# Semaphore raises carried by VectorE's own instructions, and a sort, a weighing and sums in smaller pieces, in a four-layer graph network kernel

## What is computed

```python
h = relu(layernorm(x)); x = x + relu(norm_adj @ (h @ W0))            # layer 0, D^-1/2 (A+I) D^-1/2
h = relu(layernorm(x)); x = x + cat(h, g@h, g@g@h, g@g@g@h) @ W.T + b # layer 1, g likewise
h = relu(layernorm(x)); x = x + mlp(h + quantile_agg(h, dilate(adj))) # layer 2
h = relu(layernorm(x)); x = x + adj @ (h @ W3) + b3                   # layer 3
```

## Time and profile before

| | |
|---|---|
| median of three runs | 1851.67 us (1849.76 to 1852.83) |
| the profiled execution: its own time, its span | 1848.78 us, 1847.0 us |
| PE busy | 1377.5 us (75%) |
| DVE busy | 1471.5 us (80%) |
| ACT busy | 826.6 us (45%) |
| POOL busy | 1304.7 us (71%) |

### The profile page before, as it was taken

How to read it: one execution, slowest core, us unless ns; L and a number is a source line. 1 busy time by engine, 2 the same in 40 slices (tenths; PEclk the granted TensorE clock), 3 DMA queues, 4 the chain that set the end, 5 groups by cost and what they waited for, 6 DMA issues and landing times.

```text
span 1847.0 us, 26217 instructions
## 1 busy us (share of the span) xinstructions
PE 1377.5 (75%) x8997; PEld 802.5 (43%) x8997; DVE 1471.5 (80%) x2491; ACT 826.6 (45%) x2340; POOL 1304.7 (71%) x1196
## 2 busy tenths in 40 slices
PE   2878768797878788787979788787979788780404
PEld 1454435455444455445444444444544545440202
DVE  1345788889898898889898888889898988988352
ACT  5354436354454646354544546354553546230202
POOL 2027787877777777878777777778787777878720
PEclk9888869797988979797988989797988879795555
DMA  4123433324333343325344334324343433222220
GB/s 143 57 54 83 71 80 64 59 60 97 58 75 81 64 92 63 71 47 98 58 75 81 69 87 64 76 44 95 59 74 82 71 86 31 28 31 28 26 15 6
DMA packets 106625, 120.25 MB, mean 65 GB/s; under 512 B 71486, under 2 KB 71614, under 8 KB 106430
## 3 DMA queue, kind: packets, MB, share of 16 engines
q0 software_dynamic: 36864, 37.82, 20.1%
q1 hardware_dynamic: 69566, 79.98, 13.7%
HBM read 109.27 MB, written 8.45 MB: 64 GB/s over the span
## 4 chain that ended last, share of the span: by engine, by line
DVE 53%; POOL 16%; issue 12%; PE 9%; ACT 6%; DMA 4%; DVEq 1%; POOLq 0%; SPq 0%; ACTq 0%
POOL slots L436 15%; DVE lists L1281 6%; DVE slots L1101 5%; DVE slots L1100 5%; PE ps_tr L687 3%; DMA slots<-h_rows,row_no 3%; DVE slots L1176 2%; DVE stat_norm L1076 2%; DVE low L1093 2%; DVE y_mid L1092 2%; ACT h L524 2%; PE ps_tr L695 2%; ACT z_mid L514 1%; DVE y_mid L1323 1%; PE ps_prod L706 1%
## 5 line engine op out<-in xcount | busy, mean ns | idle before, releaser
L436 POOL DMA_INDIRECT slots<-h_rows,row_no x1152 | 1292.9, 1122 | 459.3 <-issue 349.0
L687 PE MATMUL ps_tr<-adj_t,y_mid 128*128 128x512 bf16 x1024 | 278.6, 415 | 44.2 <-DVEq L1094 41.5
L495 ACT ACTIVATE columns_t<-ps_tr 128x512 f32<-128x512 f32 (+1 forms) x160 | 93.2, 591 | 337.5 <-PE ps_tr L695 289.7
L1100 DVE TENSOR_TENSOR slots<-slots 128x512 f32<-128x512 f32 (+3 forms) x160 | 174.7, 1092 | 63.4 <-DMA slots<-h_rows,row_no 53.5
L514 ACT ACTIVATE h<-x,stat_norm 128x64 f32<-128x64 f32 x384 | 128.0, 335 | 142.1 <-DVEq L1078 142.1
L687 PEld LDWEIGHTS ps_tr<-adj_t,y_mid 128*128 128x128 bf16 x1024 | 100.3, 105 | 198.1 <-issue 124.2
L1101 DVE TENSOR_TENSOR slots<-slots 128x512 f32<-128x512 f32 (+3 forms) x160 | 173.3, 1083 | 0.0
L1281 DVE MAX8 lists<-ps_key 128x8 f16<-128x1024 f32 x128 | 157.8, 1233 | 17.9 <-DVE lists L1281 0.5
L660 PE MATMUL ps_tr<-ident_h,adj_n 128*128 128x128 f16 x1024 | 102.3, 266 | 80.0 <-ACT adj_t L495 40.3
L695 PE MATMUL ps_tr<-adj_t,low 128*64 128x512 bf16 x1024 | 141.6, 400 | 0.0
L549 ACT ACTIVATE merged<-xc 128x256 f32<-128x256 f32 (+2 forms) x48 | 24.2, 505 | 249.8 <-DVEq L1153 249.6
(11 more groups left out here) (210 smaller groups left out, 2546.6 us busy)
## 6 DMA issues: line engine op xcount, KB each, us to landing
adj_f<-in_adj SPq DMA_DIRECT2D x128, 512.0 KB, 4.8
slots<-h_rows,row_no POOLq DMA_INDIRECT x1152, 3.1
x<-in_x SPq DMA_DIRECT2D x16, 256.0 KB, 3.0
h_rows<-h SPq DMA_DIRECT2D x16, 256.0 KB, 4.0
out<-x SPq DMA_DIRECT2D x16, 256.0 KB, 2.6
xc<-in_L_gnn_W SPq DMA_DIRECT2D x1, 64.0 KB
w_sb<-in_L_gnn_W SPq DMA_DIRECT2D x2, 32.0 KB
h_rows<-zeros SPq DMA_DIRECT2D x2, 32.0 KB, 1.5
```

The source lines that it names most:

```text
L436: pool.indirect_dma_start(out=slots[:, slot_of(par, s), t * C:(t + 1) * C], out_offset=None, in_=table[par][:, :], in_offset=bass.Indirect ...
L495: act.activation(dst, view, ACT.Copy, scale=scale).then_inc(tr_free, 1)
L687: nc.tensor.matmul(dst[:, :], top_halves(pair_of)[:, j, :], adj_t[g % 3][:, columns[j]], start=(j == 0 and not begun), stop=False)
L1100: st.done(v.tensor_tensor(low_to, first, second, ALU.min))
```

## The change

Three things change, all of them for DVE's stream; the other engines only wait on other semaphores or counts.

- In all places but `merge` (and the branch `slow_v`, which is not taken for these inputs), the separate `sem_inc` is gone, and the instruction itself raises the semaphore of the other engine in place of `v_step`. Where DVE's next instruction needs the result, DVE now waits on that other semaphore (`key_read`, `product_read`, `wide_ready`, `slots_read`, `misc_free`); elsewhere it doesn't wait at all. Two double raises become one: `flag_ready` and `result_ready` vanish (their readers use `key_free` and `prod_free`), and `aggregate` raises only `agg_ready`.
- `sort_1` and `sort_2` of `THE_REST` run as `NARROW_2` (256 columns) and `WIDE` (128 columns) one after the other. The later stages still take `THE_REST` whole.
- `weigh_odd` and `weigh_even` take three slots in three instructions of 128 x 512, which took one of 128 x 1536; the first sum of `narrow_sum` likewise.

```diff
-        NARROW_1, THE_REST = slice(0, F // 2), slice(F // 2, COLS * C)
+        NARROW_1, NARROW_2, WIDE = slice(0, F // 2), slice(F // 2, F), slice(F, COLS * C)
+        THE_REST = slice(F // 2, COLS * C)
...
             def store_result(g):
-                sp.wait_ge(result_ready, g + 1)
+                sp.wait_ge(prod_free, PROD["lin3", g] + 1)
...
             def hidden_rows(g, i):
+                if i == 0:
+                    pe.wait_ge(agg_ready, g + 1)
                 misc_turn(f"hid.{i}", g)
...
             def norm_begin(name, g):
                 total, less_mean, _, _ = stat_of(name)
                 step(v.tensor_reduce(total, tiles(x[g % 4]), AX.X, ALU.add))
-                step(v.tensor_scalar(less_mean, total, -1.0 / C, None, ALU.mult))
-                dve.sem_inc(mean_ready, 1)
+                v.tensor_scalar(less_mean, total, -1.0 / C, None, ALU.mult).then_inc(mean_ready, 1)
...
-                step(v.tensor_tensor(last[:, :, 0:C], rest, tops[:, :, C:2 * C], ALU.subtract))
-                dve.sem_inc(parts_ready, 1)
+                v.tensor_tensor(last[:, :, 0:C], rest, tops[:, :, C:2 * C], ALU.subtract).then_inc(parts_ready, 1)
...
-            def weigh(g, first, n, wire, gap):
+            def weigh(g, at, rank):
...
             def weigh_odd(g):
-                weigh(g, 2, 3, 1, 2)
+                weigh(g, 2, 1)
+                weigh(g, 3, 3)
+                weigh(g, 4, 5)
...
-                odd, even = wires(par, 2, 3, 1, F_COLS), wires(par, 10, 3, 1, F_COLS)
-                step(v.tensor_tensor(odd, odd, even, ALU.add))
                 one, two, three, last = [wires(par, s, 1, 1, F_COLS)[:, 0, :] for s in (2, 3, 4, 15)]
+                for odd, at in ((one, 10), (two, 11), (three, 12)):
+                    st.done(v.tensor_tensor(odd, odd, wires(par, at, 1, 1, F_COLS)[:, 0, :], ALU.add))
+                st.wait()
...
+            def key_read(name, g):
+                dve.wait_ge(key_free, KEY[name, g] + 1)
...
             def row_list(g, t):
-                step(v.max(out=lists[:, t * SLOTS:(t + 1) * SLOTS], in_=read_key(f"row{t}", g)))
-                free_key()
+                v.max(out=lists[:, t * SLOTS:(t + 1) * SLOTS], in_=read_key(f"row{t}", g)).then_inc(key_free, 1)
...
             def add_layer3(g):
                 dve.wait_ge(prod_full, PROD["lin3", g] + 1)
-                step(v.tensor_tensor(x[g % 4][:, :], x[g % 4][:, :], ps_prod[:, :], ALU.add))
-                dve.sem_inc(prod_free, 1)
-                dve.sem_inc(result_ready, 1)
+                v.tensor_tensor(x[g % 4][:, :], x[g % 4][:, :], ps_prod[:, :], ALU.add).then_inc(prod_free, 1)
...
-                    sort_1(c, THE_REST)
-                    sort_2(c, THE_REST)
+                    sort_1(c, NARROW_2)
+                    sort_1(c, WIDE)
+                    sort_2(c, NARROW_2)
+                    sort_2(c, WIDE)
```

More of the change, by code:

```diff
@@ L87, in gnn_stack @@
     MISC = numbered(turns, [("c", "spread"), ("c", "hid.0"), ("c", "hid.1"), ("c", "mlp")])
+    MISC_FREED = numbered(turns, [("c", "hid.0"), ("c", "hid.1"), ("c", "mlp")])
     PROD = numbered(turns, [("d", "lin3"), ("b", "lin0"), ("b", "lin1"), ("b", "v1"), ("b", "v2"), ("b", "v3")])
@@ L651, in misc_turn @@
             def misc_turn(name, g):
-                at_least(pe, misc_free, MISC[name, g])
+                at_least(pe, misc_free, MISC_FREED[name, g])
             def transpose_adjacency(g):
@@ L782, in spread_wide @@
                 pe.wait_ge(wide_summed, g + 1)
-                misc_turn("spread", g)
+                misc_turn("hid.0", g)
                 for t in range(T):
@@ L798, in slow_pe @@
             def slow_pe(g):
-                pe.wait_ge(flag_ready, g + 1)
+                pe.wait_ge(key_free, KEY["over", g] + 1)
                 settle(pe)
@@ L981, in slow_v @@
             def slow_v(g):
-                dve.wait_ge(flag_ready, g + 1)
+                dve.wait_ge(key_free, KEY["over", g] + 1)
                 settle(dve)
@@ L1166, in wide_sum @@
                 step(v.tensor_copy(parts_w[:, 1, :], agg_w[:, :]))
-                step(v.tensor_tensor(parts_w[:, 2, :], agg_w[:, :], parts_w[:, 1, :], ALU.subtract))
-                dve.sem_inc(wide_summed, 1)
-            def weigh(g, first, n, wire, gap):
+                v.tensor_tensor(parts_w[:, 2, :], agg_w[:, :], parts_w[:, 1, :], ALU.subtract).then_inc(wide_summed, 1)
+            def weigh(g, at, rank):
                 par = g % 2
                 if par:
[L1173 to L1176, removed]
+                    rank = SLOTS - 1 - rank
+                values = tiles(wires(par, at, 1, 1, slice(0, F))[:, 0, :])
+                w = weight[g % 2][:, 0:T, rank]
+                st.done(v.tensor_tensor(values, values, over_c(w), ALU.mult))
             def weigh_odd(g):
-                weigh(g, 2, 3, 1, 2)
+                weigh(g, 2, 1)
+                weigh(g, 3, 3)
+                weigh(g, 4, 5)
             def weigh_even(g):
-                weigh(g, 10, 3, 2, 2)
+                weigh(g, 10, 2)
+                weigh(g, 11, 4)
+                weigh(g, 12, 6)
             def weigh_last(g):
-                weigh(g, 15, 1, 7, 1)
+                weigh(g, 15, 7)
             def narrow_sum(g):
@@ L1267, in wide_lists @@
                                      lost.unsqueeze(1).to_broadcast([P, LIST, 2 + SLOTS]), ALU.is_equal))
-                step(v.tensor_tensor(over_b[:, :], crowd[:, :], over[:, :], ALU.add))
-                dve.sem_inc(over_ready, 1)
+                v.tensor_tensor(over_b[:, :], crowd[:, :], over[:, :], ALU.add).then_inc(over_ready, 1)
                 st.done(v.tensor_copy(lists[:, COLS * SLOTS:COLS * SLOTS + 1], self_mask[:, 0:1]))
@@ L1313, in weights, with product_read @@
                                      scale[:, :].unsqueeze(2).to_broadcast([P, COLS, SLOTS]), ALU.mult))
+            def product_read(name, g):
+                dve.wait_ge(prod_free, PROD[name, g] + 1)
             def layer0_out(g):
                 dve.wait_ge(prod_full, PROD["lin0", g] + 1)
-                step(v.scalar_tensor_tensor(y, by_tile(ps_prod), 0.0, over_c(d0[g % 2]), ALU.max, ALU.mult))
-                dve.sem_inc(prod_free, 1)
+                v.scalar_tensor_tensor(y, by_tile(ps_prod), 0.0, over_c(d0[g % 2]), ALU.max, ALU.mult)\
+                    .then_inc(prod_free, 1)
+                product_read("lin0", g)
                 step(v.tensor_tensor(tiles(x[g % 4]), tiles(x[g % 4]), y, ALU.add))
@@ L1322, in propagate @@
                 dve.wait_ge(prod_full, PROD[name, g] + 1)
-                step(v.tensor_tensor(y, by_tile(ps_prod), over_c(d1_sq[g % 2]), ALU.mult))
-                dve.sem_inc(prod_free, 1)
+                v.tensor_tensor(y, by_tile(ps_prod), over_c(d1_sq[g % 2]), ALU.mult).then_inc(prod_free, 1)
+                product_read(name, g)
                 split(y_mid, low)
```

71 lines of the change are left out of this document (31 added, 40 removed).

## The result

| | before | after |
|---|---|---|
| median of the timed runs | 1850.7 us | 1778.8 us |
| ratio, 95% interval | | 0.961 (0.959 to 0.963) |
| profiled execution: span | 1847.0 us | 1773.8 us |
| first start of a gather issue | 123.4 us | 121.8 us |
| mean of a gather issue | 1122 ns | 1061 ns |

Forecast were 1774 us and a range of 1744 to 1815 us. The page of the kernel after, the busy line and the group of the gather; they answer to the earlier trace rows. Lines of the code have moved by a few numbers (the gather is L437, the row lists are still L1281).

What follows compares the result with a forecast made beforehand. POOL's gather and DVE together set a 103.23 us turn. Fourteen turns at 98.3 us save 69.0, then 2.5 + 1.0 + 3.4 + 0.4: -76.3 from 1848.78, 1772.5, taken as 1774 us, range 1744 to 1815 us.

Steps and rivals of the forecast that it cites:

- Both engines set the turn: POOL's gather and DVE both run almost without pauses at 103.23 us a turn, so a gain on one alone stops.
- The raises, -8.9 us of a DVE turn: Removing 45 separate raises at 42 places of DVE's turn shortens the pauses: 1.2, 7.4 and 0.3 us.
- the pieces, +0.9: On DVE, splitting two sort stages, the weighings and the sum into smaller instructions adds 0.9 us a turn.
- DVE's busy share: Sign in the profile after: DVE's busy share above 84%, where it was 80% before.
- What becomes late next, 1.8 us: New DVE waits for ACT's norm (0.7 us), layer 3's split and layer 1's output (0.4 each), and layer 1's first products.
- The holds: A gather issue starting under a DVE instruction with two SBUF tensors waits for its end, then needs 0.82 us.
- The formula for a random start: Mean hold by DVE instruction length L is (L - 0.1)^2 / 2.86; the pieces cut 6.7 to 3.3 us a gather.
- The calculation issue by issue: Walking 72 issues through the new turn's 165 DVE instructions by the 0.82 rule: 96.8 to 99.5 us, middle 98.1.
- The term for the first turn's gather: The first turn's gather, with no sort beside it, was to save 1 us.
- POOL does keep the gain: Rival, 12 in 100: DVE finishes early but pieces do not help POOL; turn 101.2 to 103 us, total 1820 us.
- PE and ACT did not take over: Rival, 13 in 100: DVE's waits on PE or ACT grow to 4 us a turn; turn 100 to 101, total 1803 us.
- Slower by step: Rival, 4 in 100: in the full-width sort, four 1.22 us pieces in a row each hold an issue 1.0 us; 1867 us.

Runs made afterwards that it cites:

- experiments 1 to 4: Parts of the change added to the kernel before: raises alone 0.990, pieces alone 1.003, raises with weighing and sum pieces 0.976, raises with sort pieces 0.972.
- raises: The changed kernel with sort, weighing and sum whole again, so only the raises carried by the instructions: 1830.8 us, 0.990 of the kernel before.
- experiment 5: Against the kernel with the raises alone, two three-slot weighings became reductions reading one SBUF tensor, the six-rank weighing left out: 1831.3 us, ratio 0.990.
- pieces: The kernel before with the smaller sort, weighing and sum instructions and nothing else, all raises separate: 1855.6 us, ratio 1.003.
- finest: The changed kernel with sort_1 and sort_2 in 128-column pieces throughout, full-width stages 3, 4, middle and 5 in 256 and 128 columns: 1758.3 us, ratio 0.950.

## Why the prediction was right

*Both engines set the turn.* Shown by experiments 1 to 4, with a sign for each half: 0.990 for one, 1.003 for the other, 0.961 for both.

*The raises, -8.9 us of a DVE turn, and the pieces, +0.9.* The gaps came as worked out (0.04 and -0.08 for 0.03 and -0.08), and a stage in pieces takes 3.72 us as summed. Over the fourteen turns DVE's turn without its wait for the gather is 103.2 - 1.1 = 102.1 us before, 102.3 - 7.8 = 94.5 in `raises` and 98.4 - 3.1 = 95.3 in the changed kernel; forecast were 97.0. Less the waits for PE and ACT (0.3, 2.0 and 1.9 us) that is -9.3 us for the raises and +0.9 for the pieces, as summed. The 97.0 were too long mostly because the sum started at the whole 103.2, DVE's 1.1 us of waiting for the gather included. One sign was missed: DVE's busy share was to pass 84% and is 82%. Two instructions that overlap by 0.08 us are busy only once in that time, and by an estimate from the 32 such places, 32 x 16 x 0.08, this takes 41 us off.

*What becomes late next, 1.8 us.* Measured 1.9 us a turn, but only partly where the forecast put it, so the total is in part luck. The split of layer 3 waits 0.38 us for ACT, as forecast (0.4). The norm's wait for ACT was to cost 0.7 and costs 0.1; DVE waits 0.75 us before that, for PE's next key matrix at the row list, and ACT is done by the time that is over.

*The holds.* The rule held for the instructions with two SBUF tensors: an issue is held by one, to its end, and needs 0.82 us from there. An instruction with one tensor holds nothing in the cases forecast, with the exception in experiment 5. The formula for a random start gives 3.4 us a gather for the pieces, and in `raises` against the changed kernel the turn differs by 3.8 us. The size was close by luck more than by right: summed from the traces, the seven long instructions held the issues for 4.5 us a gather, where the formula has 6.7, and what replaced them for 1.1, where it has 3.3. Both are 2.2 too high, and only the difference is right. The issues beside the two sorts in pieces run in step with them and are free but for one (last section), which a random start does not give, and experiment 5 shows that holds do not add. The calculation issue by issue, which keeps the order, gave 98.1 us a turn; 98.4 was measured. For the raises alone it gave 101.1 and 102.3 was measured, so it is good to about 1 us in 100.

*The sum.* Forecast against measured, in spans: the 14 turns -69.0 and -67.2 (1445.3 less 1600.39 - 222.32); up to the sort of batch 0 -3.5 and -1.9; the last gather -3.4 and -3.3 (103.0 and 99.7); the tail -0.4 and -0.8 (74.5 and 73.7). In all -76.3 and -73.2. The 3.1 us that are missing are 1.8 in the turns (98.4 for 98.3), 0.9 up to the first gather (1.6 for 2.5), 0.7 from there to the first sort and 0.1 in the last gather, less 0.4 that the tail gave beyond its term. The term for the first turn's gather had no ground: 94.2 us before and 94.3 after, where the sum had 1 us less. There is no full-width sort beside it, and the sum had allowed for a gain all the same.

*The rivals.* POOL does keep the gain of the raises, all but 19 us, if it is given them alone: this rival was right about the mechanism, and the pieces are what decided against it. PE and ACT did not take over. Slower by step did not come: instructions of 1.22 us do hold single issues (in the narrow sort, which the change left as it was, the one at 704.51 takes 1.97 us, and in ten of eleven turns the first issue beside the full-width pieces is held, see the last section), but not four in a row, and the pieces hold for less in all than the whole ones did. The rule of the Trainium skill (VectorE: DVE Perf Modes, section Rules for kernel authors), "Minimize op count, not sems", is half right here: the ten more instructions a turn do cost time where DVE is the longer one (`pieces`, 1.003), but so do separate raises (without them `raises` has 0.990).

## What to carry to other kernels

Where two engines are both without pauses, measure a change of one only together with what it lets through on the other: the same edit was worth +5 us alone and -52 us on top of its partner. Beside a GpSimd that issues indirect DMAs without a pause, as here, a VectorE instruction with two SBUF tensors can hold an issue for up to its own length, so cut the longest first, and stop when VectorE waits for the gather hardly any more: the further pieces of `finest` brought nothing. Read from the timeline which instructions hold, and do not go by the number of tensors alone. Let the instruction itself raise the other engine's semaphore: a separate raise is a pause of 0.11 to 0.12 us each here.

## What was not expected of the hardware

The hold moves. With the holds at two weighings gone entirely, the kernel took as long (1831.3 against 1830.8 us), since the freed issues arrived under other instructions; after halving one of these, 9.7 us were gained.

The hold has an edge at the start. In `raises` the second weighing of the turn catches no issue that begins with it, but is a little longer itself:

```profile
766.04 1.83 DVE L1175 TENSOR_TENSOR slots<-slots,weight 128x1536 f32<-128x1536 f32 x1
```

```profile
766.08 0.95 POOL L437 DMA_INDIRECT slots<-h_rows,row_no  x1 [0.30 <-issue]
```

The first weighing takes 1.75 us, this one 1.83. Over the twelve traces, of 214 issues that begin up to 0.03 us behind the start of an instruction with two SBUF tensors (and 0.25 us or more before its end) 4 are held, and of 665 that begin 0.06 to 0.13 us behind it all are; in between it goes both ways. In the kernel before, an issue falls 0.03 to 0.05 us behind the start of the second weighing in 15 turns. It is the one behind the issue that the first weighing held, so a hold in one place decides what the next place catches.

The issues can run clear of a dense stretch: from 715.54 to 723.98 us seven in a row took 0.94 to 0.95 us beside eight two-tensor instructions of 1.22 and 0.69 us with no gap between them. In ten of eleven turns read, five to seven issues in a row beside these two stages take 0.95 us or less (in the eleventh the five take up to 1.02), and in all but this one they come behind one that is held, for 1.17 to 1.97 us in all. The hold itself could bring this about: the freed issue ends 0.82 us behind an instruction, so the next starts at a fixed place of the next instruction, and with a step of 1.25 us and pairs of 1.22 and 0.69 us it then falls near an end each time. Three steps are 3.74 us and a stage is 3.72, so the two keep their places from one stage to the next. An issue that begins in the last 0.13 us of an instruction loses nothing, since 0.82 us behind its end is then no later than its own 0.95. No run varied the lengths alone, so this reason is argued and not shown.
